# The last normalization's scale and shift: one result tile in four moves from ScalarE to VectorE

## The chip, the cores and the metric

The kernel runs on one core of a Trainium2 chip. The metric is the device time of one execution in microseconds (us). The profiled execution is a run of its own, with its own time.

## What is computed

A graph network with 50,000 nodes of 256 features and 50,000 edges sorted by destination. A first layer (edge messages, two dense products, a batch norm) is added to x and normalized over the features; then three graph convolutions follow, and their result is added and normalized again. The change lies in the last layer and its normalization:

```python
def layer(h, W, b):
    h = h @ W.T
    msg = h[src] * norm[:, None]
    agg = jax.ops.segment_sum(msg, dst, num_segments=n)
    return jax.nn.relu(agg + b)
...
x = _layernorm(x + _L1_gnn_ref(...), axis=-1)   # (x - mean) / sqrt(var + eps)
```

## The kernel before

Each layer is one pass over the nodes. In the last pass (`last_pass`) the unit of work is a quad: 512 nodes, which are 4 tiles of 128 nodes by 256 features; there are 98 quads. Five engines work on it, each with a program of its own, tied by semaphores.

Each engine repeats a step (`quad_pipeline`, unrolled by four). `at(n)` in a step is the quad that entered the pipeline n steps ago, so one step of an engine does a part of several quads at different ages. The order inside a step is the order of the code, and an engine takes its instructions in that order. In brief, with the age of the quad in brackets:

- GpSimd (POOL) issues five indirect DMAs for a quad, which gather up to 608 rows of the layer before from HBM into `rows`, a ring of four quads. It has no step; it waits for `rows_ready` of the quad four back (L489 to L496).
- ScalarE (ACT): relu of the product, `h_ps` [5]; rounding of the sums to `agg_hi` [3]; four squares with their sums, `spread` [6]; rounding of the gathered rows to `rows_hi` [1]; the square root `sd` [6]; the four result tiles `y` [7] (L1680).
- VectorE (DVE): `rs` = 1/sd [7]; five select matrices [1] (L510); `shift` [7]; the four sums `res` = x1 * degree + h [5] (L1605); `agg_lo` [3]; `less_mean` [5]; `power` [6]; the five remainders `rows_lo` [1] (L1633), which release the matrix products and GpSimd.
- TensorE (PE): the dense product [4] of 28 matmuls, then eight transposes and the 20 matmuls that sum the gathered rows [2].
- SyncE (SP) issues the loads of `own` [0] and of `x1` [2], and the store of `y` [8], each of 512 KB.

The result of one tile is y = res * rs + shift, with rs and shift one number for each row. `y` has two buffers, so its writer waits for the store of the quad two back (`stored`).

Of the kernel before, what the change touches and what calls it, by code (L numbers as in the profile page):

```python
# [47 lines left out]
QUAD_RING = GROUP // 2  # L48
# [9 lines left out]
ALU = mybir.AluOpType  # L58
# [393 lines left out]
def quad_rows(dram, q):  # L452

    return dram[bass.ds(q * QUAD, QUAD), :].rearrange("(j p) d -> p j d", p=P)


def quad_block(dram, q):

    return dram[bass.ds(q, 1)].rearrange("o p j d -> p (o j) d")
# [7 lines left out]
def load_quad(sp, fast, out, source, base, quad, landed, slot_free):  # L467

    for ran, rows in ((1, source), (0, base)):
        with sp.If(fast == ran):  # L470
            if quad.has(QUAD_RING):
                sp.wait_ge(slot_free, quad.before(QUAD_RING))
            sp.dma_start(out, quad_rows(rows, quad.q)).then_inc(landed, 16)


def load_root_rows(sp, c, dram, quad, landed):

    sp.dma_start(c["root_row"][0:3, quad.slot].bitcast(F32), dram["root_rows"][:, bass.ds(quad.q * QUAD, QUAD)])\
        .then_inc(landed, 16)
# [26 lines left out]
def select_columns(nc, c, quad, select, blocks=range(BLOCKS)):  # L506

    for b in blocks:
        first, end = SPAN[b]
        last = nc.vector.tensor_scalar(select[:, b, 0:end - first], c["iota32"][:, first:end],  # L510
                                       c["place"][:, bass.ds(quad.q, 1), b], None, ALU.is_equal)
    return last
# [983 lines left out]
def last_pass(nc, keep, dram, source, layer, weight):  # L1496

    c = keep
    with ExitStack() as stack:
# [8 lines left out]
        res = m.sb("fin_res", [P, QUAD_RING, 4, D])  # L1508
        spread = m.sb("fin_spread", [P, 2, 4, D])
        y = m.sb("fin_y", [P, 2, 4, D])  # L1510
# [5 lines left out]
        rs = m.sb("fin_rs", [P, 2, 4])  # L1516
        shift = m.sb("fin_shift", [P, 2, 4])
# [4 lines left out]
        gathered = [m.sem(f"fin_gathered{s}") for s in range(QUAD_RING)]  # L1522
        stored = [m.sem(f"fin_stored{b}") for b in range(2)]
        names = ("rows_rounded rows_ready agg_done agg_rounded agg_split dense_done h_ready res_added "
                 "mean_ready squared power_ready sd_ready shift_ready y_ready")
        (rows_rounded, rows_ready, agg_done, agg_rounded, agg_split, dense_done, h_ready, res_added,
         mean_ready, squared, power_ready, sd_ready, shift_ready, y_ready) = (
            m.sem("fin_" + n) for n in names.split())

        with nc.Block() as block:  # L1530

            @block.sync
            def _(sp):
                fast = sp.value_load(c["fast_i"][0:1, 0:1], min_val=0, max_val=1)

                def step(at):
                    if quad := at(0):
                        load_quad(sp, fast, own[:, quad.slot], source, dram["base"], quad, loaded[quad.slot], agg_done)
                    if quad := at(2):
                        s = quad.slot  # L1540
                        if quad.has(QUAD_RING):
                            sp.wait_ge(res_added, quad.before(QUAD_RING))
                        sp.dma_start(x1[:, s], quad_rows(dram["x1"], quad.q)).then_inc(x1_in[s], 16)
                        load_root_rows(sp, c, dram, quad, x1_in[s])
                    if quad := at(8):
                        sp.wait_ge(y_ready, quad.done())
                        sp.dma_start(quad_block(dram["out"], quad.q), y[:, quad.b]).then_inc(stored[quad.b], 16)

                quad_pipeline(sp, step)
                for b in range(2):  # L1550
                    sp.wait_ge(stored[b], 16 * (NQ // 2))
# [26 lines left out]
            @block.vector  # L1578
            def _(dve):

                def step(at):
                    if quad := at(7):
                        b = quad.b
                        dve.wait_ge(sd_ready, quad.done())
                        if quad.has(2):
                            dve.wait_ge(y_ready, quad.before(2))
                        nc.vector.reciprocal(rs[:, b], sd[:, b]).then_inc(shift_ready, 1)
                    if quad := at(1):
                        if quad.has(2):
                            dve.wait_ge(agg_done, quad.before(2))  # L1590
                        select_columns(nc, c, quad, select[:, quad.b])
                    if quad := at(7):
                        b = quad.b
                        dve.wait_ge(shift_ready, quad.done(2) - 1)
                        nc.vector.tensor_tensor(shift[:, b], less_mean[:, b], rs[:, b], ALU.mult).then_inc(shift_ready, 1)
                    if quad := at(5):
                        b, s = quad.b, quad.slot
                        dve.wait_ge(h_ready, quad.done())
                        dve.wait_ge(x1_in[s], quad.landed(2))
                        if quad.has(QUAD_RING):  # L1600
                            dve.wait_ge(y_ready, quad.before(QUAD_RING))
                        if quad.has(2):
                            dve.wait_ge(mean_ready, quad.before(2))
                        for j in range(4):
                            last = nc.vector.scalar_tensor_tensor(  # L1605
                                out=res[:, s, j], in0=x1[:, s, j], scalar=c["deg"][:, quad.tile(j)],
                                in1=h_ps[:, b, j], op0=ALU.mult, op1=ALU.add, accum_out=total[:, b, j:j + 1])
                        last.then_inc(res_added, 1)
                    if quad := at(3):
                        b = quad.b  # L1610
                        dve.wait_ge(agg_rounded, quad.done())
                        nc.vector.tensor_tensor(agg_lo[:, b], agg_ps[:, b], agg_hi[:, b].bitcast(F32), ALU.subtract)\
                            .then_inc(agg_split, 1)
                    if quad := at(5):
                        b = quad.b
                        dve.wait_ge(res_added, quad.done())
                        if quad.has(2):
                            dve.wait_ge(shift_ready, quad.before(2) * 2)
                        nc.vector.tensor_scalar(less_mean[:, b], total[:, b], -1.0 / D, None, ALU.mult)\
                            .then_inc(mean_ready, 1)  # L1620
                    if quad := at(6):
                        b = quad.b
                        dve.wait_ge(squared, quad.done())
                        if quad.has(2):
                            dve.wait_ge(sd_ready, quad.before(2))
                        nc.vector.scalar_tensor_tensor(out=power[:, b], in0=c["deg"][:, bass.ds(quad.q * 4, 4)],
                                                       scalar=LN_EPS * D, in1=squares[:, b], op0=ALU.mult, op1=ALU.add)\
                            .then_inc(power_ready, 1)
                    if quad := at(1):
                        b, s = quad.b, quad.slot  # L1630
                        dve.wait_ge(rows_rounded, quad.done())
                        for k in range(BLOCKS):
                            last = nc.vector.tensor_tensor(rows_lo[:, b, k], c["rows"][:, s, k],  # L1633
                                                           rows_hi[:, b, k].bitcast(F32), ALU.subtract)
                        last.then_inc(rows_ready, 1)

                quad_pipeline(dve, step)

            @block.scalar
            def _(act):  # L1640
                def step(at):
                    if quad := at(5):
                        b = quad.b
                        act.wait_ge(dense_done, quad.done())
                        nc.scalar.activation(h_ps[:, b], h_ps[:, b], ACT.Relu).then_inc(h_ready, 1)  # L1645
                    if quad := at(3):
                        b = quad.b
# [4 lines left out]
                    if quad := at(6):  # L1652
                        b = quad.b
# [8 lines left out]
                    if quad := at(1):  # L1662
                        b, s = quad.b, quad.slot
# [4 lines left out]
                    if quad := at(6):  # L1668
                        b = quad.b
# [4 lines left out]
                    if quad := at(7):  # L1674
                        b, s = quad.b, quad.slot
                        act.wait_ge(shift_ready, quad.done(2))  # L1676
                        if quad.has(2):
                            act.wait_ge(stored[b], quad.twos * 16)  # L1678
                        for j in range(4):
                            last = nc.scalar.activation(y[:, b, j], res[:, s, j], ACT.Identity,  # L1680
                                                        bias=shift[:, b, j:j + 1], scale=rs[:, b, j:j + 1])
                        last.then_inc(y_ready, 1)

                quad_pipeline(act, step)


# [84 lines left out]
```

## Time and profile before

| | us |
|---|---|
| median of three runs | 3808.47 (3804.52 to 3809.65) |
| the profiled execution | 3810.63 |
| its span, first to last instruction | 3808.9 |
| the last pass in it, first rounding to the end | 3091.9 to 3808.9 |

Of the span, PE was busy 87%, ACT 74%, DVE 74% and POOL 66%, but these are averages over passes that differ. From 3300 to 3700 us, in the last pass, ACT is busy 100.00 us of each 100 and DVE 87.65 to 89.56. An instruction's time in the trace is from its start to its end, and two of one engine may overlap; what an instruction costs its engine is therefore read from start to start.

### The profile page before, as it was taken

To read this page: it belongs to the slowest core of one execution; us is meant where nothing else is said; L and a number is where in the kernel's file an instruction comes from. 1 tells how busy PE (TensorE), PEld (TensorE's weight loads), DVE (VectorE), ACT (ScalarE), POOL (GpSimd) and SP (SyncE) were. 2 spreads that over 40 slices of the span, in tenths; PEclk is the share of its full clock that TensorE was granted. 3 is DMA by queue.
4 is the path that set the end of the run, shared out by engine and by line. 5 is a ranking of instruction groups with operands and counts; after the bars stand their busy time and mean duration, and the time that the engine had idled before them with its cause. 6 is when DMAs were issued, how large, how long until landed. Compare 5 with 4: busy or idle time off the path is not lost. (4 is left out here: it accounts for less than half of the span.)

```text
span 3808.9 us, 89464 instructions
## 1 busy us (share of the span) xinstructions
PE 3296.5 (87%) x25134; PEld 3161.6 (83%) x25134; DVE 2833.9 (74%) x7975; ACT 2835.5 (74%) x5811; POOL 2495.6 (66%) x2663
## 2 busy tenths in 40 slices
PE   3999999999999344447999999799999979999997
PEld 2999999999998344336999999799999979999997
DVE  4888888888886777774666666466666658888887
ACT  1666666666665578875878888578888859999999
POOL 4666666666662666646777777577777757777773
PEclk7999999999999555558999999999999989999999
DMA  3555555555552799996777777577777769999996
GB/s 94 160 161 165 164 162 164 165 162 161 166 162 96 265 344 343 339 322 196 242 233 238 240 238 224 182 239 237 237 240 238 235 196 303 303 296 302 296 299 212
DMA packets 654363, 858.86 MB, mean 225 GB/s; under 512 B 136335, under 2 KB 515882, under 8 KB 654256
## 3 DMA queue, kind: packets, MB, share of 16 engines
q1 hardware_dynamic: 556954, 652.14, 52.5%
q0 software_dynamic: 94080, 205.08, 19.3%
q10 hardware_dynamic: 3222, 0.43, 0.1%
q8 instruction: 41, 0.67, 0.1%
q14 instruction: 66, 0.54, 0.0%
HBM read 639.00 MB, written 257.52 MB: 235 GB/s over the span
## 5 line engine op out<-in xcount | busy, mean ns | idle before, releaser
L494 POOL DMA_INDIRECT rows<-gb_scratch,node_i x490 | 502.0, 1024 | 200.3 <-issue 133.5
L494 POOL DMA_INDIRECT rows<-x_scratch,node_i x490 | 500.1, 1021 | 187.6 <-issue 131.3
L494 POOL DMA_INDIRECT rows<-x_in,node_i x490 | 512.5, 1046 | 165.0 <-issue 124.4
L494 POOL DMA_INDIRECT rows<-ga_scratch,node_i x490 | 499.2, 1019 | 176.7 <-issue 129.2
L510 DVE TENSOR_SCALAR gcn_select<-iota,place 128x256 fp32r<-128x256 f32 (+2 forms) x980 | 367.8, 375 | 217.6 <-ACT gcn_rows_hi L1482 214.6
L526 PE MATMUL gcn_agg_ps<-gcn_select,gcn_rows_hi 128*128 128x256 f32 (+2 forms) x1960 | 502.5, 290 | 17.0 <-DVE gcn_rows_lo L1453 17.0
L540 PE MATMUL gcn_h_ps<-g_hi,gcn_agg_hi 128*128 128x256 f32 x1568 | 457.0, 291 | 63.7 <-ACT gcn_h_ps L1468 62.4
L526 PE MATMUL gcn_agg_ps<-gcn_select,gcn_rows_lo 128*128 128x256 f32 (+2 forms) x1960 | 484.1, 287 | 0.0
L988 ACT ACTIVATE h1t<-h1t_ps,b_sb 128x256 f32<-128x256 f32 x392 | 164.6, 471 | 423.8 <-PE h2t_ps L591 418.3
L540 PE MATMUL gcn_h_ps<-g_lo,gcn_agg_hi 128*128 128x256 f32 x1568 | 445.8, 284 | 0.0
L540 PE MATMUL gcn_h_ps<-g_hi,gcn_agg_lo 128*128 128x256 f32 x1568 | 445.0, 284 | 0.0
L1444 DVE TENSOR_TENSOR gcn_agg_lo<-gcn_agg_ps,gcn_agg_hi 128x1024 fp32r<-128x1024 f32 x196 | 240.0, 1225 | 272.6 <-ACT gcn_agg_hi L1476 272.6
L1196 POOL TENSOR_SCALAR hot_node<-iota,node_in_tile 128x128 bf16<-128x128 f16 x490 | 286.7, 611 | 203.7 <-PE deg_ps L1251 144.7
L1453 DVE TENSOR_TENSOR gcn_rows_lo<-rows,gcn_rows_hi 128x256 fp32r<-128x256 f32 x980 | 404.7, 413 | 0.0
L924 POOL TENSOR_TENSOR attr_lo<-attr,attr_hi 128x384 fp32r<-128x384 f32 x196 | 190.7, 974 | 307.6 <-ACT attr_hi L1012 305.5
L1482 ACT CAST gcn_rows_hi<-rows 128x1280 fp32r<-128x1280 f32 x196 | 247.4, 1262 | 190.3 <-DMA rows<-ga_scratch,node_i 95.2
L526 PEld LDWEIGHTS gcn_agg_ps<-gcn_select,gcn_rows_hi 128*128 128x128 f32 x1960 | 374.3, 191 | 17.4 <-DVE gcn_rows_lo L1453 17.4
L526 PEld LDWEIGHTS gcn_agg_ps<-gcn_select,gcn_rows_lo 128*128 128x128 f32 x1960 | 375.4, 192 | 0.0
L591 PE MATMUL h2t_ps<-h1t,w 128*128 128x256 f32 x1568 | 370.5, 379 | 2.8 <-ACT h2t L998 2.8
L571 PE MATMUL agg_ps<-gin_select,msg_hi 128*128 128x256 f32 (+1 forms) x1372 | 349.1, 294 | 18.2 <-DVE msg_lo L1109 14.6
L540 PEld LDWEIGHTS gcn_h_ps<-g_hi,gcn_agg_hi 128*128 128x128 f32 x1568 | 298.7, 191 | 76.1 <-issue 74.3
L1468 ACT ACTIVATE gcn_h_ps<-gb_sb,root_degree 128x256 f32<-128x256 f32 x784 | 327.9, 464 | 23.3
(191 smaller groups left out, 11461.0 us busy)
## 6 DMA issues: line engine op xcount, KB each, us to landing
own<-x_t_in SPq DMA_DIRECT2D x196, 256.0 KB, 2.7
h_scratch<-h2t SPq DMA_DIRECT2D x196, 256.0 KB, 2.9
h2t_in<-h_scratch SPq DMA_DIRECT2D x98, 512.0 KB, 5.1
x_sb<-x_q_in SPq DMA_DIRECT2D x98, 512.0 KB, 6.9
x_scratch<-x SPq DMA_DIRECT2D x98, 512.0 KB, 5.6
gcn_own<-x_scratch SPq DMA_DIRECT2D x98, 512.0 KB
ga_scratch<-gcn_h SPq DMA_DIRECT2D x98, 512.0 KB, 3.3
gcn_own<-ga_scratch SPq DMA_DIRECT2D x98, 512.0 KB
```

What stands on the lines that cost most here:

```text
L494: pool.indirect_dma_start(out=c["rows"][0:n, slot, b], out_offset=None, in_=source[:, :], in_offset=bass.IndirectOffsetOnAxis(ap=c["node"] ...
L510: last = nc.vector.tensor_scalar(select[:, b, 0:end - first], c["iota32"][:, first:end], c["place"][:, bass.ds(quad.q, 1), b], None, ALU.i ...
L526: last = nc.tensor.matmul(out[:, h, first:end], rows[:, b, k, h * P:(h + 1) * P], select[:, b, k, 0:end - first], start=False, stop=k == B ...
L540: last = nc.tensor.matmul(out[:, j], tile_columns(a[:, h], j), w[:, h], start=False, stop=n == len(terms) - 1, skip_group_check=layer is None)
L571: last = nc.tensor.matmul(out[:, h, first:end], rows[:, pair.odd + b, h * P:(h + 1) * P], select[:, b, first:end], start=h == 0 and b == 0 ...
L591: last = nc.tensor.matmul(out[:, m], w[:, h, m * P:(m + 1) * P], a[:, h], start=n == 0, stop=n == len(terms) - 1)
L924: nc.gpsimd.tensor_tensor(attr_lo[:, q % 2, 0:columns], attr[:, q % GROUP, 0:columns], attr_hi[:, q % 2, 0:columns].bitcast(F32), ALU.subt ...
L1196: last = nc.gpsimd.tensor_scalar(hot_node[:, quad % 2, b], c["iota16"][:, 0:P], node_in_tile[:, quad, b:b + 1], None, ALU.is_equal)
L1444: nc.vector.tensor_tensor(agg_lo[:, b], agg_ps[:, b], agg_hi[:, b].bitcast(F32), ALU.subtract)\
L1453: last = nc.vector.tensor_tensor(rows_lo[:, b, k], c["rows"][:, s, k], rows_hi[:, b, k].bitcast(F32), ALU.subtract)
L1468: last = nc.scalar.activation(h_ps[:, quad.b, j], bias[:], ACT.Identity, scale=c["root"][:, quad.tile(j)])
L1482: nc.scalar.copy(rows_hi[:, b], c["rows"][:, s]).then_inc(rows_rounded, 1)
```

## The change

ScalarE computes three of the four `y` tiles of a quad. VectorE computes the fourth with one `tensor_scalar` (multiply, then add, both numbers per row), as the last piece of its step. A new semaphore, `fourth_ready`, tells of it: the store waits for it beside `y_ready`, and so does the piece that overwrites `res` four quads later.

```diff
@@ SyncE, the store @@
                     if quad := at(8):
                         sp.wait_ge(y_ready, quad.done())
+                        sp.wait_ge(fourth_ready, quad.done())
                         sp.dma_start(quad_block(dram["out"], quad.q), y[:, quad.b]).then_inc(stored[quad.b], 16)
@@ VectorE, ahead of res @@
                         if quad.has(QUAD_RING):
                             dve.wait_ge(y_ready, quad.before(QUAD_RING))
+                            dve.wait_ge(fourth_ready, quad.before(QUAD_RING))
@@ VectorE, end of the step @@
                         last.then_inc(rows_ready, 1)
+                    if quad := at(7):
+                        b, s = quad.b, quad.slot
+                        dve.wait_ge(shift_ready, quad.done(2))
+                        if quad.has(2):
+                            dve.wait_ge(stored[b], quad.twos * 16)
+                        nc.vector.tensor_scalar(y[:, b, 3], res[:, s, 3], rs[:, b, 3:4], shift[:, b, 3:4],
+                                                ALU.mult, ALU.add).then_inc(fourth_ready, 1)
@@ ScalarE @@
-                        for j in range(4):
+                        for j in range(3):
                             last = nc.scalar.activation(y[:, b, j], res[:, s, j], ACT.Identity,
                                                         bias=shift[:, b, j:j + 1], scale=rs[:, b, j:j + 1])
```

VectorE in the full part of the pass, at the border of two steps, before:

```order
L1626 SCALAR_TENSOR_TENSOR fin_power<-degree,fin_squares 128x4
L1633 TENSOR_TENSOR fin_rows_lo<-rows,fin_rows_hi 128x256 x5
L1587 RECIPROCAL fin_rs<-fin_sd 128x4
L510 TENSOR_SCALAR fin_select<-iota,place 128x256 x2
L510 TENSOR_SCALAR fin_select<-iota,place 128x320
```

And in the changed kernel:

```order
L1628 SCALAR_TENSOR_TENSOR fin_power<-degree,fin_squares 128x4
L1635 TENSOR_TENSOR fin_rows_lo<-rows,fin_rows_hi 128x256 x5
L1643 TENSOR_SCALAR fin_y<-fin_res,fin_rs,fin_shift 128x256
L1588 RECIPROCAL fin_rs<-fin_sd 128x4
L510 TENSOR_SCALAR fin_select<-iota,place 128x256 x2
L510 TENSOR_SCALAR fin_select<-iota,place 128x320
```

One instruction stands between `rows_lo` and the next step's `rs`; nothing else on VectorE changes place. ScalarE at the end of a step, before:

```order
L1667 CAST fin_rows_hi<-rows 128x1280
L1673 ACTIVATE fin_sd<-fin_power 128x4
L1680 ACTIVATE fin_y<-fin_res,fin_shift,fin_rs 128x256 x4
L1645 ACTIVATE fin_h_ps<-fin_h_ps 128x1024
L1651 CAST fin_agg_hi<-fin_agg_ps 128x1024
```

And in the changed kernel:

```order
L1676 CAST fin_rows_hi<-rows 128x1280
L1682 ACTIVATE fin_sd<-fin_power 128x4
L1689 ACTIVATE fin_y<-fin_res,fin_shift,fin_rs 128x256 x3
L1654 ACTIVATE fin_h_ps<-fin_h_ps 128x1024
L1660 CAST fin_agg_hi<-fin_agg_ps 128x1024
```

The last of the four `y` tiles is gone, and the order is the same.

## Rows read from the trace of the kernel before

**Rows 1.** Busy time by stretch: PE, PEld, DVE, ACT, POOL, clock, DMA share, GB/s

```profile
1500.00:1700.00 200.00, 93.57 (x562) 81.78 (x562) 155.26 (x644) 161.14 (x319) 120.59 (x208) 0.55 0.98 344
...
3500.00:3600.00 100.00, 97.22 (x797) 95.49 (x796) 89.56 (x328) 100.00 (x228) 71.29 (x72) 1.00 0.95 299
```

**Rows 2.** What ACT waited for, 3132 us to the end

```profile
ACT fin_rows_hi L1667 <- DMA rows<-gb_scratch,node_i: 1.6, 1, 1.6
ACT fin_sd L1673 <- DVE fin_power L1626: 1.1, 5, 0.2
```

**Rows 3.** Timeline of ACT, one step: start, length, engine, line

```profile
3504.68 1.48 ACT L1667 CAST fin_rows_hi<-rows 128x1280 fp32r<-128x1280 f32 x1
3505.83 0.43 ACT L1673 ACTIVATE fin_sd<-fin_power 128x4 f32<-128x4 f32 x1
3505.93 2.30 ACT L1680 ACTIVATE fin_y<-fin_res,fin_shift,fin_rs 128x256 f32<-128x256 f32 x4
3507.90 1.23 ACT L1645 ACTIVATE fin_h_ps<-fin_h_ps 128x1024 f32<-128x1024 f32 x1
...
3511.73 1.48 ACT L1667 CAST fin_rows_hi<-rows 128x1280 fp32r<-128x1280 f32 x1
```

**Rows 4.** Groups of DVE by line, 3137 to 3772 us (90 steps)

```profile
L1633 DVE TENSOR_TENSOR fin_rows_lo<-rows,fin_rows_hi 128x256 fp32r<-128x256 f32 x450 | 159.1, 420 | 69.8 <-ACT fin_rows_hi L1667 69.8
```

**Rows 5.** Timeline of DVE: five rows_lo, then the first, second and fourth select

```profile
3506.18 1.77 DVE L1633 TENSOR_TENSOR fin_rows_lo<-rows,fin_rows_hi 128x256 fp32r<-128x256 f32 x5 [0.76 <-ACT fin_rows_hi L1667]
...
3507.96 0.33 DVE L510 TENSOR_SCALAR fin_select<-iota,place 128x256 fp32r<-128x256 f32 x1
...
3508.20 0.65 DVE L510 TENSOR_SCALAR fin_select<-iota,place 128x256 fp32r<-128x256 f32 x2
...
3508.77 0.58 DVE L510 TENSOR_SCALAR fin_select<-iota,place 128x256 fp32r<-128x256 f32 x1
```

**Rows 6.** Timelines of ACT and DVE at two hand-overs between them

```profile
3173.18 1.26 ACT L1667 CAST fin_rows_hi<-rows 128x1280 fp32r<-128x1280 f32 x1
...
3174.47 1.77 DVE L1633 TENSOR_TENSOR fin_rows_lo<-rows,fin_rows_hi 128x256 fp32r<-128x256 f32 x5 [0.71 <-ACT fin_rows_hi L1667]
...
3791.78 0.16 DVE L1626 SCALAR_TENSOR_TENSOR fin_power<-degree,fin_squares 128x4 f32<-128x4 f32 x1
...
3791.97 0.20 ACT L1673 ACTIVATE fin_sd<-fin_power 128x4 f32<-128x4 f32 x1 [0.23 <-DVE fin_power L1626]
```

**Rows 7.** Timeline of POOL: gathers of quads 8, 34, 48 and 49

```profile
3133.71 1.09 POOL L494 DMA_INDIRECT rows<-gb_scratch,node_i  x1 [0.30 <-issue]
...
3309.66 1.20 POOL L494 DMA_INDIRECT rows<-gb_scratch,node_i  x1 [0.30 <-issue]
...
3402.56 1.03 POOL L494 DMA_INDIRECT rows<-gb_scratch,node_i  x1 [0.30 <-issue]
...
3409.42 1.02 POOL L494 DMA_INDIRECT rows<-gb_scratch,node_i  x1 [0.44 <-DVE fin_rows_lo L1633]
```

**Rows 8.** Timeline of DVE beside the second of those gathers

```profile
3308.56 1.77 DVE L1633 TENSOR_TENSOR fin_rows_lo<-rows,fin_rows_hi 128x256 fp32r<-128x256 f32 x5 [0.78 <-ACT fin_rows_hi L1667]
```

**Rows 9.** Timeline of PE at the border of two steps

```profile
3504.96 0.27 PE L526 MATMUL fin_agg_ps<-fin_select,fin_rows_lo 128*128 128x128 f32 x1
3505.34 0.39 PE L536 MATMUL fin_h_ps<-bias_row,root_row 128*128 128x256 f32 x1
3505.57 0.28 PE L540 MATMUL fin_h_ps<-g_hi,fin_agg_hi 128*128 128x256 f32 x1
3505.68 0.28 PE L540 MATMUL fin_h_ps<-g_hi,fin_agg_lo 128*128 128x256 f32 x1
```

**Rows 10.** DMA issues by line, and SP's timeline at one store

```profile
x_sb<-x_q_in SPq DMA_DIRECT2D x98, 512.0 KB, 6.9
...
3501.34 0.37 SPq L1547 DMA_DIRECT2D out<-fin_y  x1
```

**Rows 11.** Timeline of ACT at the end: last y tiles

```profile
3801.74 4.02 ACT L1680 ACTIVATE fin_y<-fin_res,fin_shift,fin_rs 128x256 f32<-128x256 f32 x8
```

More of the change, by code:

```diff
@@ L1524, in last_pass @@
         names = ("rows_rounded rows_ready agg_done agg_rounded agg_split dense_done h_ready res_added "
-                 "mean_ready squared power_ready sd_ready shift_ready y_ready")
+                 "mean_ready squared power_ready sd_ready shift_ready y_ready fourth_ready")
         (rows_rounded, rows_ready, agg_done, agg_rounded, agg_split, dense_done, h_ready, res_added,
-         mean_ready, squared, power_ready, sd_ready, shift_ready, y_ready) = (
+         mean_ready, squared, power_ready, sd_ready, shift_ready, y_ready, fourth_ready) = (
             m.sem("fin_" + n) for n in names.split())
```

## The prediction

> **What bounds the kernel now.** I began with the busy time by stretch. In the last pass ACT is busy all of the time, and the DMA engines 95% of it [rows 1]. "Busy" doesn't prove a bound, so the waits came next: from 3132 us to the end ACT waits once for a gather, 1.6 us, and five times for `power`, 1.1 us together [rows 2]. An engine that never waits sets the pace. The timeline gives that pace: from one `rows_hi` to the next 3511.73 - 3504.68 = 7.05 us [rows 3]. DVE, in contrast, waits in each step for `rows_hi`: 69.8 us over 90 steps, 0.775 us each [rows 4]. So DVE's own work is 7.05 - 0.78 = 6.28 us (unrounded).
>
> ACT's pace holds for about 90 steps. Ahead of 3132 us gathers arrive late and ACT waits for them; at the end the pipeline drains.
>
> **What the change removes.** The four `y` tiles take from 3505.93 to the next start at 3507.90, 1.97 us, so one takes 0.49 [rows 3]. ACT alone would need 7.05 - 0.49 = 6.56 us for a step. If nothing else came up, 90 x 0.49 = 44 us would go. The question is what holds the step before it gets down to 6.56.
>
> **What it adds.** One `tensor_scalar` of 128x256 from SBUF to SBUF on DVE. The trace has the same operation with one scalar, the selects. The first and second of them start 0.24 us apart (3507.96, 3508.20) [rows 5]. The fourth lasts 0.58 instead of 0.33 us, and so costs some 0.24 + 0.25 = 0.49 [rows 5]. The `rows_lo` pieces, two tensors in, cost 1.69 / 5 = 0.34 each (3506.18 to the `rs` ahead of 3507.96). I take 0.28, near the low end since the operation is that of the selects, and keep 0.24 to 0.49 for the range. A second scalar might cost something; no row shows one. DVE alone then needs 6.28 + 0.28 = 6.56 us (6.52 to 6.77).
>
> The Trainium skill (VectorE: DVE Perf Modes, the perf-mode tier table) has fp32 `tensor_scalar` between SBUF tensors at twice the rate of `tensor_tensor`. The 0.24 beside 0.34 points the same way; by the full rate of one element a cycle it would be near the 0.34, which lies within the range.
>
> The added waits should cost nothing: `shift_ready` was raised in the same DVE step, and the store of two quads back is long landed. That store goes out at 3501.34 [rows 10], and its buffer is written again two steps on, at 3505.93 + 7.05 = 3512.98 [rows 3]: 11.6 us later. Of the 512 KB transfers on the page with a landing time the longest took 6.9 [rows 10]. If this cover were gone, DVE would stand ahead of `rs`, and with it the selects and `res`. SP's store now waits for `fourth` too, which ends some 0.3 us after `rows_lo` (3506.18 + 1.77), at 3508.2; SP's next store before was at 3501.34 + 7.05 = 3508.4, so it goes out no later than it did.
>
> **What holds the step then.** Four candidates lie within 0.15 us of each other.
>
> *A loop through ACT and DVE.* `rows_hi` releases `rows_lo`; after it, in DVE's order, come the fourth tile and all work up to `power` of the next step; `power` releases `sd`, and behind `sd` ACT does `y`, relu, `agg_hi`, the squares and `rows_hi`. That is two steps round. Its terms: `rows_hi` to `rows_lo` 1.29 [rows 6]; `rows_lo` to the end of the next `power` 6.28, since DVE idles only ahead of `rows_lo` [rows 4], plus 0.28; hand-over to `sd` 0.03 (3791.78 + 0.16 to 3791.97) [rows 6]; `sd` to `rows_hi` 3511.73 - 3505.83 = 5.90 [rows 3], less 0.49. Sum 13.29, 6.65 a step (6.63 to 6.75). Before, the same loop takes 13.50, 6.75 a step, and so was covered by 7.05. Here is a first part of the gain that is not had: both engines will wait for each other a little in each step.
>
> *POOL.* A quad is five gathers. From the first gather of quad 8 at 3133.71 to that of quad 48 at 3402.56 POOL never waits: 268.85 / 40 = 6.72 us a quad [rows 7]. Then the ring is full and POOL waits for `rows_lo` [rows 7]. At 3132 us ACT has no lead of gathers at all; it used to gain 0.33 us a quad only by being slower than POOL. With ACT faster than 6.72, each step waits for its gather. That makes 6.72 a floor.
>
> *PE.* The last matmul of a step and the first of the next start 0.38 apart, where 0.12 is usual, and the second follows 0.23 later instead of 0.11 [rows 9]. Without that wait PE would need 7.05 - 0.26 - 0.12 = 6.67.
>
> *DMA.* The share is 0.95 [rows 1], so a quad is 0.95 of 7.05, 6.70 us of transfer work. The highest share for long is 0.98, in another pass, at 344 GB/s [rows 1]. At such a share the step is 6.84.
>
> I take 6.77 us, between POOL's 6.72 and the 6.84 of DMA. **The sum:** 90 x (7.05 - 6.77) = 25 us. In the drain, from the last full steps on, ACT has seven more sets of `y`, the last two together as eight tiles from 3801.74 [rows 11]; one tile less each is at most 7 x 0.49 = 3.4, of which I take 2.5, since the fourth tile of the last quad still has to come from DVE behind its `shift`. Together 28. Against the profiled execution that is 3810.6 - 28 = 3782.6; the median of the runs lies 2.2 us under it, so 3780.5, rounded to 3781.
>
> **Rivals.**
>
> *Gathers get slower still.* Unhindered gathers last about 1.02 us, but one in five lasts some 0.2 more, as that of 3309.66 with 1.20 [rows 7], which lies beside `rows_lo` of 3308.56 to 3310.33 [rows 8]. If the added operation, which follows `rows_lo` at once, hinders a gather in the same way, POOL needs 6.92 a quad: 90 x 0.13 + 2.5 = 14 us, 3794. For it: it falls into the time when POOL is issuing. Against: it is short beside the 1.69 of `rows_lo`, and the selects, of its kind, are themselves stretched to 0.58 [rows 5]. The Trainium skill (GPSIMD Engine Reference, specifications) says that GpSimd's SBUF interfaces are shared with VectorE and contended by two-port modes and by two SBUF inputs. By that rule this rival comes true as soon as the contention falls on POOL. Chance 0.17.
>
> *The floor of POOL is softer than it looks,* for instance since gathers that wait for `rows_lo` don't collide with it: 3409.42 follows `rows_lo` and lasts 1.02 [rows 7]. Then the loop decides, 6.65: 90 x 0.40 + 3 = 39 us, 3769. Against: POOL has to be ahead before it waits. Chance 0.05.
>
> *Nothing is won.* If the transfers are already at their limit with 0.95, ACT's relief turns into waits for loads, and 3806 or so stays. Against: ACT waited for none [rows 2]. Chance 0.07.
>
> *Slower.* The fourth tile stands at DVE's busiest place, ahead of `rs`, selects and `res`. If it costs more than DVE's slack of 0.78 plus 0.08, some 0.86 us, each step grows beyond 7.14 and the time beyond the 0.2%. Waiting for a store that lands more than 11 us after its issue, on engines 98% busy, would do that: at 1.0 us, 90 x 0.23 less 2.5 is 18 us, 3827. Against: the landings above. Chance 0.05.
>
> **How the numbers follow.** The forecast, a step of 6.69 to 6.85 and so 18 to 36 us, has 0.66. About 0.2% (7.6 us) is what a measurement tells from no change; the first, second and third cases lie below 3800.9 almost whole, so faster 0.87, same 0.08, slower 0.05. The range reaches from 3773, where the step is POOL's floor (30) with all of the drain and a little more, to 3797, behind the slower gathers. The likeliest case's own range is 3773 to 3790.
>
> **What would show it.** In the profile after: `y` on ACT 294 times and on DVE 98 times. The period from `rows_hi` to `rows_hi` near 6.77, not 6.56. ACT is no longer without waits: it waits for `power` ahead of `sd`, and in the first 40 quads for gathers. DVE's wait ahead of `rows_lo` falls from 0.78 to some 0.2 or 0.3. POOL seldom or never waits for `rows_lo`, and gathers come without pause at 6.72. The DMA share is 0.98 or more. The start-to-start cost of the fourth tile is 0.24 to 0.34. I'd be wrong if the fourth tile shows a wait for a store, if POOL's period between two quads grows to 6.9, or if ACT still never waits and the period is 6.56.

## The result and the profile after

The changed kernel takes 3768.12 us (median of four runs, 3765.84 to 3769.79), the kernel before 3809.06 in the same comparison. The ratio is 0.9892, interval 0.9875 to 0.9909: 1.1% less time. The forecast was 3781, its range 3773 to 3797.

The profiled span went from 3808.9 to 3768.0 us, 40.9 less. The timeline of ACT shows where; these are the roundings of quads 0, 8, 40 and 97, each with its start and length:

```profile
3089.88 1.26 ACT L1676 CAST fin_rows_hi<-rows 128x1280 fp32r<-128x1280 f32 x1 [16.59 <-DMA rows<-gb_scratch,node_i]
...
3142.34 1.26 ACT L1676 CAST fin_rows_hi<-rows 128x1280 fp32r<-128x1280 f32 x1 [0.28 <-DMA rows<-gb_scratch,node_i]
...
3357.68 1.25 ACT L1676 CAST fin_rows_hi<-rows 128x1280 fp32r<-128x1280 f32 x1
...
3735.63 1.25 ACT L1676 CAST fin_rows_hi<-rows 128x1280 fp32r<-128x1280 f32 x1
```

The same four in the kernel before:

```profile
3091.90 1.26 ACT L1667 CAST fin_rows_hi<-rows 128x1280 fp32r<-128x1280 f32 x1 [16.83 <-DMA rows<-gb_scratch,node_i]
...
3144.97 1.25 ACT L1667 CAST fin_rows_hi<-rows 128x1280 fp32r<-128x1280 f32 x1
...
3370.67 1.39 ACT L1667 CAST fin_rows_hi<-rows 128x1280 fp32r<-128x1280 f32 x1
...
3772.72 1.58 ACT L1667 CAST fin_rows_hi<-rows 128x1280 fp32r<-128x1280 f32 x1
```

| stretch | before | after | less |
|---|---|---|---|
| up to quad 0's rounding (code not changed) | 3091.9 | 3089.9 | 2.0 |
| quad 0 to 8 | 53.1 | 52.5 | 0.6 |
| quad 8 to 97, 89 steps | 627.8 | 593.3 | 34.5 |
| quad 97 to the end | 36.2 | 32.4 | 3.8 |

The 2.0 us come from code that is the same in both. In the ten experiments below, with the same code up to that point, it lies anywhere from 3081.6 to 3096.7. For that reason the experiments are judged by their steps in the last pass, and their times only in support.

The step was 7.05 us all through. Now it is (3357.68 - 3142.34) / 32 = 6.73 us up to quad 40 and (3735.63 - 3357.68) / 57 = 6.63 behind it. The groups of DVE, 3140 to 3725 us, to be read against [rows 4]:

```profile
L1635 DVE TENSOR_TENSOR fin_rows_lo<-rows,fin_rows_hi 128x256 fp32r<-128x256 f32 x439 | 155.3, 420 | 21.8 <-ACT fin_rows_hi L1676 21.1
...
L1643 DVE TENSOR_SCALAR fin_y<-fin_res,fin_rs,fin_shift 128x256 f32<-128x256 f32 x87 | 35.4, 407 | 0.0
```

DVE waits 21.1 us over 88 steps for `rows_hi`, 0.24 each, where it was 0.78. Ahead of the fourth tile it shows no idle time (the 0.0), so the added wait for the store cost nothing. One step of DVE and the hand-overs to ACT in the timeline, for [rows 5] and [rows 6]:

```profile
3497.88 0.15 DVE L1628 SCALAR_TENSOR_TENSOR fin_power<-degree,fin_squares 128x4 f32<-128x4 f32 x1
3498.20 1.77 DVE L1635 TENSOR_TENSOR fin_rows_lo<-rows,fin_rows_hi 128x256 fp32r<-128x256 f32 x5 [0.18 <-ACT fin_rows_hi L1676]
3499.89 0.41 DVE L1643 TENSOR_SCALAR fin_y<-fin_res,fin_rs,fin_shift 128x256 f32<-128x256 f32 x1
3500.21 0.17 DVE L1588 RECIPROCAL fin_rs<-fin_sd 128x4 f32<-128x4 f32 x1
3500.30 1.54 DVE L510 TENSOR_SCALAR fin_select<-iota,place 128x256 fp32r<-128x256 f32 x5
3501.55 0.28 DVE L1596 TENSOR_TENSOR fin_shift<-fin_less_mean,fin_rs 128x4 f32<-128x4 f32 x1
```

```profile
3496.92 1.25 ACT L1676 CAST fin_rows_hi<-rows 128x1280 fp32r<-128x1280 f32 x1
3498.14 0.20 ACT L1682 ACTIVATE fin_sd<-fin_power 128x4 f32<-128x4 f32 x1
3498.30 1.59 ACT L1689 ACTIVATE fin_y<-fin_res,fin_shift,fin_rs 128x256 f32<-128x256 f32 x3
3499.79 1.00 ACT L1654 ACTIVATE fin_h_ps<-fin_h_ps 128x1024 f32<-128x1024 f32 x1
...
3503.61 1.25 ACT L1676 CAST fin_rows_hi<-rows 128x1280 fp32r<-128x1280 f32 x1
3504.76 0.20 ACT L1682 ACTIVATE fin_sd<-fin_power 128x4 f32<-128x4 f32 x1
```

The fourth tile costs DVE 3500.21 - 3499.89 = 0.32 us, start to start. `sd` comes 1.22 us after `rows_hi`, where it was 1.15 [rows 3], and 0.11 after the end of `power`: In the next step it comes after 3504.76 - 3503.61 = 1.15. So it goes on: from quad 40 to 95 `sd` comes later than 1.16 us in 27 of 55 steps, every other one, and steps of about 6.57 and 6.70 us take turns. ACT is thus held a little at `sd` in every second step, although the view of waits doesn't count it, since the instruction before still runs. That is what a loop over two steps would do. The five selects take 3501.55 - 3500.30 = 1.25 us.

Busy time by stretch, with the same columns as [rows 1], for both parts of the pass:

```profile
3140.00:3350.00 210.00, 208.69 (x1749) 208.30 (x1748) 202.27 (x751) 207.57 (x471) 161.85 (x159) 1.00 0.98 314
3402.00:3720.00 318.00, 318.00 (x2679) 318.00 (x2678) 306.14 (x1152) 318.00 (x721) 244.85 (x241) 1.00 0.97 317
```

PE no longer has an idle moment in the second part. The timeline of PE shows its own pace, by the transposes of quads 40 and 95:

```profile
3362.06 1.03 PE L520 MATMUL fin_agg_ps<-ident,fin_own 128*128 128x128 f32 x8
...
3727.99 1.04 PE L520 MATMUL fin_agg_ps<-ident,fin_own 128*128 128x128 f32 x8
```

That is (3727.99 - 3362.06) / 55 = 6.653 us. PE is thus a little slower than ACT's 6.63 and uses up a lead on the way. The gathers of POOL, grouped, 3402 to 3720 us:

```profile
L494 POOL DMA_INDIRECT rows<-gb_scratch,node_i x241 | 246.3, 1022 | 73.5 <-issue 73.5
```

Five of them take 5 x (246.3 + 73.5) / 241 = 6.635 us. The same group for the part of the pass before, 3137 to 3402 us:

```profile
L494 POOL DMA_INDIRECT rows<-gb_scratch,node_i x200 | 204.5, 1023 | 61.0 <-issue 60.6 <-DVE fin_rows_lo L1635 0.3
```

That is 5 x 265.5 / 200 = 6.64 us a quad there as well, although ACT's step is 6.73: from quad 8's rounding to quad 40 ACT shows waits for gathers only twice, 0.3 and 1.4 us.

Behind quad 40 ACT and DVE, PE, and POOL are within 0.02 us of each other, and each could be what holds the step. The experiments take them apart.

### The profile page after: what moved, and what is told of

The parts are those of the page before. It is cut to its first block and busy times, and to the rows that moved or that the text cites. A ratio compares the mean times of both kernels' runs of the same rounds, so it can differ in the third digit from the quotient of the medians.

```text
span 3768.0 us, 89700 instructions
## 1 busy us (share of the span) xinstructions
PE 3275.6 (87%) x25134; PEld 3151.0 (84%) x25134; DVE 2851.4 (76%) x8073; ACT 2795.7 (74%) x5713; POOL 2491.0 (66%) x2663
## 5 line engine op out<-in xcount | busy, mean ns | idle before, releaser
L494 POOL DMA_INDIRECT rows<-gb_scratch,node_i x490 | 500.7, 1022 | 178.4 <-issue 148.4
```

The costliest lines, as they stand in the source:

```text
L494: pool.indirect_dma_start(out=c["rows"][0:n, slot, b], out_offset=None, in_=source[:, :], in_offset=bass.IndirectOffsetOnAxis(ap=c["node"] ...
```

## The experiments

**The tile in DVE's gap.** The piece with the fourth tile is moved ahead of `rows_lo`, where DVE waits anyway.

```diff
                     if quad := at(7):
+                        ... the fourth tile, as it was ...
                     if quad := at(1):
                         dve.wait_ge(rows_rounded, quad.done())
                         ... rows_lo ...
-                    if quad := at(7):
-                        ... the fourth tile ...
```

> The fourth tile stands ahead of rows_lo on VectorE instead of behind it, in the gap where VectorE waits for rows_hi (0.24 us a step in the changed kernel). It then lies outside the loop from rows_hi through rows_lo, the next power and sd back to rows_hi, whose sum falls by 0.32 over two steps, 0.16 a step. Theory 1, the loop alone holds the step (6.64 us in the second half of the pass): the step falls to ScalarE's own 6.56, and the time by 6 to 9 us to about 3760. Theory 2, TensorE with its own 6.65 us holds it as well: the step stays at 6.65 and the time within 3 us of 3768. Theory 3, GpSimd's gathers hold it (6.64 a quad): the same as theory 2, but with ScalarE waiting for gathers more often.

Measured: 3766.79 us, ratio to the kernel before 0.9894 (0.9876 to 0.9912), no difference from the changed kernel's 0.9892. ACT's timeline, quads 8, 40 and 97:

```profile
3143.38 1.26 ACT L1676 CAST fin_rows_hi<-rows 128x1280 fp32r<-128x1280 f32 x1 [1.15 <-DMA rows<-gb_scratch,node_i]
...
3354.30 1.25 ACT L1676 CAST fin_rows_hi<-rows 128x1280 fp32r<-128x1280 f32 x1
...
3733.26 1.25 ACT L1676 CAST fin_rows_hi<-rows 128x1280 fp32r<-128x1280 f32 x1
```

Up to quad 40 the step is 6.59, and then 6.65, TensorE's 6.653 to the hundredth. With the loop lightened ACT uses up TensorE's lead and then goes at TensorE's pace.

**Without the bias matmuls.** PE alone is lightened.

```diff
-        if layer is not None:
+        if layer is not None and layer != 2:
             nc.tensor.matmul(out[:, j], c["root_row"][...], c["bias_row"][:, layer], start=True, stop=False)
...
-                                    start=False, stop=n == len(terms) - 1, skip_group_check=layer is None)
+                                    start=layer == 2 and n == 0, stop=n == len(terms) - 1,
+                                    skip_group_check=layer is None)
```

> The changed kernel without the 4 bias matmuls of a quad in the last pass (the bias of the last layer is left out): TensorE needs 0.48 us less a step, 6.17. Theory 1, the loop holds: the step stays near 6.64, and the time within 3 us of 3768. Theory 2, TensorE holds it: the step falls to ScalarE's 6.56 to 6.6, 4 to 8 us less. Theory 3, gathers: no change.

Measured: 3764.98 us, ratio 0.9890 (0.9874 to 0.9907). The step behind quad 40 is 6.64:

```profile
3356.52 1.25 ACT L1677 CAST fin_rows_hi<-rows 128x1280 fp32r<-128x1280 f32 x1
...
3735.04 1.25 ACT L1677 CAST fin_rows_hi<-rows 128x1280 fp32r<-128x1280 f32 x1
```

PE waits again: between 3140 and 3725 us it waits 41 times for `agg_lo`, 9.8 us. Nothing is won. So TensorE alone doesn't hold the step either.

**Both together.** The tile in the gap and no bias matmuls.

> Both together: the fourth tile ahead of rows_lo, and the 4 bias matmuls of a quad left out. Loop 6.47 or less, TensorE 6.17. If loop and TensorE are the two that hold the step, it falls to ScalarE's 6.56 and the time by 7 to 9 us, to 3760. If gathers hold it, by GpSimd's issue of 6.64 a quad, it stays within 3 us of 3768.

Measured: 3759.90 us, ratio 0.9875 (0.9859 to 0.9892).

```profile
3352.43 1.25 ACT L1677 CAST fin_rows_hi<-rows 128x1280 fp32r<-128x1280 f32 x1
...
3727.75 1.28 ACT L1677 CAST fin_rows_hi<-rows 128x1280 fp32r<-128x1280 f32 x1
```

The step is 375.32 / 57 = 6.58. Behind quad 40 either change alone gives nothing, both give 0.05 us a step; the medians of the three, taken in one comparison, agree (3766.79, 3764.98, 3759.90). So behind quad 40 the changed kernel is held by the loop of ACT and DVE at 6.63, and right above it by TensorE at 6.65. What holds this kernel shows in ACT's timeline:

```profile
3503.89 1.25 ACT L1677 CAST fin_rows_hi<-rows 128x1280 fp32r<-128x1280 f32 x1
3505.04 0.20 ACT L1683 ACTIVATE fin_sd<-fin_power 128x4 f32<-128x4 f32 x1
...
3510.47 1.26 ACT L1677 CAST fin_rows_hi<-rows 128x1280 fp32r<-128x1280 f32 x1
```

`sd` follows `rows_hi` after 1.15 us, and does so in each of the 55 steps from quad 40 to 95 (1.148 to 1.153), as in the kernel before (1.148 to 1.152), and ACT shows no idle time there. So ACT is held by nothing, and 6.58 is its own pace with three tiles; the 6.56 of prediction and expectation was 0.02 short. Here the five gathers of a quad went faster too, which the prediction's floor didn't allow for (groups of POOL, 3402 to 3720 us):

```profile
L494 POOL DMA_INDIRECT rows<-gb_scratch,node_i x243 | 246.1, 1013 | 74.0 <-issue 74.0
```

That is 5 x 320.1 / 243 = 6.59 us a quad.

**Two tiles on DVE, two on ACT.**

```diff
-                        nc.vector.tensor_scalar(y[:, b, 3], ...).then_inc(fourth_ready, 1)
+                        for j in (2, 3):
+                            last = nc.vector.tensor_scalar(y[:, b, j], ...)
+                        last.then_inc(fourth_ready, 1)
...
-                        for j in range(3):
+                        for j in range(2):
```

> VectorE computes two of the four tiles at the end of its step, ScalarE two. ScalarE's own work is 6.07 us, VectorE's 6.42 + 0.32 = 6.74 plus what contention gives. Theory 1: the loop's sum falls by 0.17 over two steps, but VectorE alone needs 6.74, so the step grows from 6.64 to 6.74 or 6.8 and the time by 7 to 13 us to about 3778. Theory 2 or 3, TensorE or the gathers hold the step: it grows less, since they are at 6.65; still VectorE's 6.74 would show in the step.

Measured: 3771.01 us, ratio 0.9907 (0.9891 to 0.9924). The time grew by 3 us, not by the 7 to 13 expected. The step behind quad 40 is (3740.52 - 3357.01) / 57 = 6.73, as worked out for DVE alone. What ACT waits for, 3140 to 3735 us:

```profile
ACT fin_sd L1684 <- DVE fin_power L1628: 40.2, 84, 0.9
```

ACT is now the one that waits, for `power`, in nearly every step. By the step, one tile on DVE is better than two; the times alone don't tell them apart, since the intervals of the ratios overlap.

**Nobody computes the fourth tile.** ACT has three; DVE's piece is left out.

```diff
-                        nc.vector.tensor_scalar(y[:, b, 3], res[:, s, 3], ...).then_inc(fourth_ready, 1)
```

> Nobody computes the fourth tile (it is left out and stays zero): ScalarE has three, VectorE none. Against the changed kernel this is the price of the tile on VectorE. VectorE's own step is 6.1 to 6.2 us, the loop 6.48, ScalarE 6.56, TensorE 6.65. Theory 2 (loop and TensorE lie side by side): TensorE's 6.65 holds the step, and the time is within 3 us of the changed kernel, 3765 to 3768: the tile on VectorE costs next to nothing. If GpSimd's gathers had a floor at 6.72, the step would be 6.72 and the time 4 us more.

Measured: 3771.69 us, ratio 0.9904 (0.9888 to 0.9921); its four runs lie apart, 3759.38 to 3773.82, and the trace is of the fastest. By the step behind quad 40, (3724.54 - 3345.69) / 57 = 6.65, it is at TensorE's pace, as in the first experiment. Neither that step nor the median is below the changed kernel's, so no cost of the tile on DVE shows behind quad 40.

**Everything but gathers and transfers lightened.** ACT computes two tiles, DVE none, and the bias matmuls are left out.

> ScalarE computes two tiles and VectorE none (tiles three and four are left out), and the four bias matmuls of a quad are left out too. ScalarE needs 6.07 us, VectorE 6.2, the loop 6.25, TensorE 6.17. What then holds the step is what lies outside them: gathers or transfers. By the prediction's floor of the gathers, 6.72, the step would stay at 6.7. If a gather's extra length is only a collision whose place shifts with the step, five unhindered gathers of 1.00 + 0.305 give 6.53, with one collision 6.7. By transfers (share 0.97 at a step of 6.63) the floor is 6.5 at a share of 0.99. I expect 6.5 to 6.6, 3755 to 3762, and ScalarE waiting for gathers in most steps.

Measured: 3772.45 us, ratio 0.9901 (0.9885 to 0.9918). The step behind quad 40 is (3742.93 - 3362.40) / 57 = 6.68, above my 6.5 to 6.6, and the time above my 3755 to 3762. What ACT waited for, 3140 to 3735 us, and the groups of POOL, 3402 to 3720 us:

```profile
ACT fin_rows_hi L1671 <- DMA rows<-gb_scratch,node_i: 33.6, 32, 1.9
```

```profile
L494 POOL DMA_INDIRECT rows<-gb_scratch,node_i x239 | 246.8, 1033 | 72.9 <-issue 68.3 <-DVE fin_rows_lo L1634 4.6
```

ACT waits for gathers 32 times in some 90 steps (I had expected most of them), and a quad of gathers takes 5 x 319.7 / 239 = 6.69 us. So the gathers do bound the step, close to where the prediction had them, but only once all else is lighter than in the changed kernel.

**The same with less to transfer.** In addition three of the four tiles of `x1` aren't loaded.

```diff
-                        sp.dma_start(x1[:, s], quad_rows(dram["x1"], quad.q)).then_inc(x1_in[s], 16)
+                        sp.dma_start(x1[:, s, 0:1], quad_rows(dram["x1"], quad.q)[:, 0:1]).then_inc(x1_in[s], 16)
```

> As the kernel before it in this list, with a quarter of x1 loaded (three of the four tiles of x1 are left out), 384 KB a quad less. If transfers hold the floor, the step falls by up to 15%, to ScalarE's and VectorE's 6.2; if GpSimd's issue of the gathers holds it, it stays at 6.5.

Measured: 3769.97 us, ratio 0.9906 (0.9881 to 0.9930). Busy time from 3400 to 3600 us:

```profile
3400.00:3600.00 200.00, 189.16 (x1551) 187.40 (x1550) 184.41 (x693) 185.64 (x420) 154.27 (x151) 0.99 0.81 257
```

The DMA share is down to 0.81, and the step behind quad 40 is (3733.38 - 3353.11) / 57 = 6.67, as in the sixth experiment; the 6.5 expected for that case didn't come. What ACT waits for there is thus the gathers at POOL's pace, not the load of the transfer engines.

**Four gathers instead of five** in the changed kernel, so that POOL has time to spare.

```diff
-                gather_quads(nc, pool, c, source, gathered, rows_ready, 1)
+                gather_quads(nc, pool, c, source, gathered, rows_ready, 1, blocks=BLOCKS - 1)
```

> The changed kernel with four gathers of five in the last pass (the rows of the fifth block are left out). GpSimd needs 5.2 us a quad and runs ahead until the ring is full, so ScalarE's waits for gathers in the first 40 quads go: 3 us less if those are what makes the first part slower (6.73 against 6.63 us a step). Against it: GpSimd then waits for rows_lo, and its gathers begin just behind it, over the selects, as in the second half of the kernel before, where the selects were stretched by 0.13 to 0.18 us a step. Then the loop grows by 0.05 to 0.09 and the second part is slower than 6.63: 6.67 to 6.72. Sum within 4 us of 3768.

Measured: 3762.22 us, ratio 0.9879 (0.9862 to 0.9895). ACT's timeline, quads 0, 8, 40 and 97:

```profile
3085.17 1.26 ACT L1676 CAST fin_rows_hi<-rows 128x1280 fp32r<-128x1280 f32 x1 [15.64 <-DMA rows<-gb_scratch,node_i]
...
3132.63 1.26 ACT L1676 CAST fin_rows_hi<-rows 128x1280 fp32r<-128x1280 f32 x1
...
3345.85 1.25 ACT L1676 CAST fin_rows_hi<-rows 128x1280 fp32r<-128x1280 f32 x1
...
3724.88 1.26 ACT L1676 CAST fin_rows_hi<-rows 128x1280 fp32r<-128x1280 f32 x1
```

From quad 0 to 8 it needs 47.5 us instead of 52.5, less than any kernel with five gathers (51.3 to 55.1), and behind quad 40 6.65 a step. The gathers thus cost the changed kernel at the start of the pass, and nothing behind quad 40. Between quad 8 and 40 it needs 6.66 a step instead of 6.73, but that says little: in the two experiments that follow, which have all five gathers, the same stretch goes at 6.68 and 6.66. The slower second part that I expected, 6.67 to 6.72, didn't come.

**More to transfer.** The changed kernel with one more load of 128 KB in each step, which nobody reads.

```diff
+                        sp.dma_start(extra[:, s:s + 1], quad_rows(dram["x1"], quad.q)[:, 0:1]).then_inc(x1_in[s], 16)
                         load_root_rows(sp, c, dram, quad, x1_in[s])
```

> The changed kernel with one more load in each step of the last pass: 128 KB of x1 a second time, to a buffer that nobody reads (6% more to transfer a quad; the output stays whole). The prediction took the transfers at 6.70 us a quad and their ceiling at a share of 0.98; the step of 6.63 has refuted the 6.84 that came of it. If transfers still have room (512 KB at 340 GB/s and more is 1.5 us, so 128 KB some 0.38 us, on top of 0.97 x 6.65 = 6.47), they need 6.85 us, and with nothing hidden the step grows to 6.85 and the time by 18 us. If the share is no measure of the work, since packets get shorter under pressure, the step stays near 6.65 and the time within 4 us of 3768.

Measured: 3769.49 us, ratio 0.9890 (0.9873 to 0.9906), the same as without it. Busy time, 3400 to 3600 us:

```profile
3400.00:3600.00 200.00, 200.00 (x1682) 199.96 (x1681) 193.19 (x724) 199.69 (x452) 154.28 (x151) 1.00 1.02 335
```

335 GB/s instead of 317, a DMA share of 1.02, and a step behind quad 40 of (3734.36 - 3355.33) / 57 = 6.65, where 6.63 was without the load and 6.85 was feared. The transfers had room.

**Less to transfer.** The changed kernel with a quarter of `x1` loaded, as above.

> The changed kernel with a quarter of x1 loaded (three of its four tiles are left out), 384 KB a quad less. If transfers hold the changed kernel's step at all, it falls to ScalarE's 6.56 to 6.6 and the time by 4 to 7 us; if loop, TensorE and the gathers' issue hold it, it stays at 6.63 to 6.65, and only the waits for gathers in the first 40 quads shrink (up to 3 us less).

Measured: 3769.36 us, ratio 0.9893 (0.9876 to 0.9909). The share is 0.83, and the step behind quad 40 (3731.35 - 3353.23) / 57 = 6.63, that of the changed kernel. Transfers don't hold it there.

## Why the prediction was wrong

**The direction was right, and so was the first half of the mechanism.** ACT bounded the pass; one tile less frees 0.47 us a step (7.05 - 6.58, the third experiment; I had 0.49), and the whole of it didn't come back because other bounds lie close beneath. Of it, 0.42 came behind quad 40 and 0.32 ahead of it. Which bound holds the step was wrong.

**The step that failed is "I take 6.77 us, between POOL's 6.72 and the 6.84 of DMA".** The step is 6.67 on average over the 89 steps, so the term "90 x (7.05 - 6.77) = 25" measured 34.5, over 89 steps. What held the step behind quad 40 was the loop of ACT and DVE, at 6.63, with TensorE at 6.65. Both ends of my choice were off:

- *Transfers at 6.84.* This was the larger fault. I multiplied the DMA share by the step and took that as a quad's fixed work, and the highest share seen elsewhere as a ceiling. Neither holds. The share times the step fell from 6.70 to 0.97 x 6.63 = 6.43 us with the same bytes, and the extra load took the share to 1.02 with a step of 6.65. The row that gave the ceiling spoke against it: a quad's 299 x 7.05, some 2108 KB, need only 6.13 us at the 344 GB/s of [rows 1]. Without that end I'd have chosen 6.72 at most.
- *POOL's 6.72 as a floor.* The number was rightly read, but it is the pace of gathers of which one in five is longer [rows 7], and the share of those isn't fixed. In the changed kernel a quad's gathers take 6.64 us in either part, in the kernel with the tile in the gap and no bias matmuls 6.59. The first 40 quads did go at 6.73, but that is not the floor: the gathers there came at 6.64, and with the tile in the gap, all five gathers in place, the same stretch went at 6.59, which a floor at 6.72 doesn't allow. Of the 0.10 by which this stretch is slower than the next, ACT's one wait of 1.4 us for a gather makes 0.04 a step; the rest wasn't taken apart.

**The loop of ACT and DVE was sized well:** 6.65 worked out, 6.63 measured behind quad 40, and shown as the bound by the second experiment against the third. Its terms moved against each other. The tile costs 0.32, not 0.28, and the hand-over to `sd` 0.11 in the step shown, where I had 0.03 from a single one. On the other side DVE's other work got shorter: from the first select to `shift` it is 1.29 us on the mean of 88 steps, and was 1.42. **TensorE's 6.67** measured 6.653.

**The drain** gave 3.8 us, not 2.5; even 7 x 0.49 = 3.4 was a little low. 2.0 us lie ahead of the pass, in code that is the same, and are no gain of the change.

**The rivals.** Slower gathers, 6.92 a quad, didn't come: they got faster. The Trainium skill's rule of shared SBUF interfaces (GPSIMD Engine Reference, specifications) would have given this rival; the traces agree for `rows_lo`, which has two inputs from SBUF: in the changed kernel, quads 8 to 89, 44 gathers last over 1.1 us, all of them among the 164 that overlap `rows_lo`, and none among the other 246 (before, quads 8 to 47: 38 of 77, and none of 123). But that is one gather in ten where it was one in five, so it didn't grow with the added operation. The soft floor with 3769 (chance 0.05) came out nearly as it was written, the loop deciding at 6.65; I had held against it that POOL must be ahead before it waits, yet POOL doesn't need to wait to be faster. The range ended at 3773, where POOL's floor was; it should have reached to this rival.

**What stays open:** why, behind quad 40, a quad's gathers take just as long as a step where they aren't the bound (6.73 in the kernel with two tiles on DVE, 6.635 in the changed one), though POOL waits for nothing there. A collision that recurs once a step and whose length shifts with the phase would do that, and the traces fit it: from quad 40 to 89 it is the third gather of a quad that is long in the changed kernel (1.12 us on the mean, the others 0.96 to 1.03), and the second in the kernel with two tiles (1.21). No run isolates it.

## What to carry to other kernels

When the bounding engine is relieved, list the next bounds and treat each as a number of its own: the engine's work, the loops of hand-overs over several steps, and TensorE's pace without its waits were each right to some 0.02 us here. A DMA share near one is no bound by itself; look whether anybody waits for a transfer, and at the rate in bytes; if nobody waits and another stretch shows a higher rate, keep it out of the sum. A pace read off while an engine collides with others is one of its paces, not a floor.

## What was not expected of the hardware

The same 2 MB a quad took 0.95 of a 7.05 us step and 0.97 of one of 6.63, and 6% more bytes were moved in an equal step at 335 GB/s with a share of 1.02. A gather's issue on GpSimd takes 1.00 us, in the changed kernel over 1.1 only where it overlaps `rows_lo` on VectorE; the mean over the second part of the pass was 1013 ns in the third experiment, 1022 in the changed kernel and 1033 in the sixth experiment, with the same gathers in each. With the same operands VectorE's five selects took 1.42 us on the mean before and 1.29 after.
